# A Mamba mixer inside a MetaFormer kernel: items ahead of the scan, taps by fewer transfers

## The reference

```python
xz = in_proj(normed)                       # x and gate, 1x1
x  = silu(depthwise_conv3x3(x)); g = silu(gate)
xm, z = split(m_in_proj(x))
xm = silu(causal_conv1d(xm, 3 taps) + b)
dt = softplus(xm @ (xp_dt @ dt_w) + dt_b)  # B, C = xm @ xp
h[t] = exp(dt * A) * h[t-1] + dt * x * B   # over 3136 pixels of an image
y = (C . h + D * xm) * silu(z)
out = out_proj(m_out_proj(y) * g)
```

## Time and profile before

| | us |
|---|---|
| median of three runs (3843.79 to 3852.31) | 3848.09 |
| profiled execution | 3854.38 |
| its span | 3852.5 |
| TensorE, VectorE, ScalarE, GpSimd busy | 3198.3, 2774.0, 2555.0, 1635.8 |
| TensorE's granted clock, mean | 0.948 |

### The profile page before, as it was taken

The page is one execution under the profiler, slowest core; times in us unless marked ns, Lnnn a source line. Parts: engine busy times, 40 slices in busy tenths (PEclk is TensorE's granted clock), DMA queues, the critical chain, the costliest instruction groups (busy, mean ns, idle before and its releaser), DMA issues. The chain is left out here.

```text
span 3852.5 us, 71476 instructions
## 1 busy us (share of the span) xinstructions
PE 3198.3 (83%) x20904; PEld 1809.4 (47%) x20904; DVE 2774.0 (72%) x4460; ACT 2555.0 (66%) x4684; POOL 1635.8 (42%) x1502
## 2 busy tenths in 40 slices
PE   5799999978677898989999765877888858688865
PEld 2688888854233343434444321333433324377722
DVE  2566666657408999989999994666999967544456
ACT  4455555559698988989898642785665629644456
POOL 0233333310047888989898863003766730000000
PEclk9899999989898999999999997998999979899979
DMA  4100000012256657574766522220000002410022
GB/s 96 28 14 14 14 14 14 14 27 59 75 140 186 160 165 197 145 200 134 208 160 188 149 64 73 49 51 22 22 21 20 18 22 58 94 39 17 17 54 53
DMA packets 210810, 298.02 MB, mean 77 GB/s; under 512 B 75034, under 2 KB 195150, under 8 KB 210258
## 3 DMA queue, kind: packets, MB, share of 16 engines
q1 hardware_dynamic: 201066, 286.08, 28.7%
q10 hardware_dynamic: 9576, 10.08, 1.1%
HBM read 193.93 MB, written 102.03 MB: 77 GB/s over the span
## 5 line engine op out<-in xcount | busy, mean ns | idle before, releaser
L1586 POOL TENSOR_TENSOR mam_hc<-mam_h,mam_cs 128x896 f32<-128x896 f32 x336 | 703.1, 2093 | 188.0 <-DVE mam_h L1551 87.0
L1551 DVE TENSOR_TENSOR_SCAN mam_h<-mam_a,mam_kept,mam_dbx 128x448 f32<-128x448 f32 x672 | 738.4, 1129 | 24.4 <-ACT mam_a L1437 23.3
L1318 PE MATMUL mam_ps_y<-mam_hc,mam_ident 128*128 128x448 f32 x1344 | 570.3, 558 | 133.1 <-POOL mam_hc L1586 132.9
L1987 POOL TENSOR_TENSOR scan_ch<-scan_h,scan_cs 128x392 f32<-128x392 f32 x256 | 339.8, 1346 | 399.6 <-DVE scan_h L1931 320.6
L1437 ACT ACTIVATE mam_a<-mam_ft,mam_a_neg 128x448 f32<-128x448 f32 x672 | 410.6, 660 | 81.0 <-DVE mam_h L1551 80.3
L1318 PEld LDWEIGHTS mam_ps_y<-mam_hc,mam_ident 128*128 128x128 f32 x1344 | 249.0, 193 | 433.4 <-POOL mam_hc L1586 224.0
L1538 DVE TENSOR_TENSOR mam_dbx<-mam_ps_u,mam_bs 128x448 f32<-128x448 f32 x672 | 381.7, 613 | 35.6 <-DMA mam_bs<-dram_bc 35.6
L766 POOL TENSOR_TENSOR att_prob<-att_prob,att_share 128x588 f32<-128x588 f32 x128 | 151.7, 1185 | 452.0 <-DVE att_share L951 452.0
L418 PE MATMUL f_xc_ff<-all_x,f_centre 128*128 (+1 forms) x256 | 125.9, 575 | 133.1 <-DVE all_x L308 133.1
L886 ACT ACTIVATE att_pt<-att_ps_t 128x512 f32<-128x512 f32 x128 | 76.5, 598 | 209.9 <-PE att_ps_t L827 209.9
L379 ACT ACTIVATE f_h<-f_hid 96x784 f16<-96x784 f32 x256 | 207.1, 811 | 0.0
(11 more groups left out here) (216 smaller groups left out, 7361.8 us busy)
## 6 DMA issues: line engine op xcount, KB each, us to landing
mam_taps<-normed SPq DMA_DIRECT2D x1008, 43.5 KB
mam_bs<-dram_bc SPq DMA_DIRECT2D x28, 896.0 KB, 14.7
mam_cs<-dram_bc SPq DMA_DIRECT2D x28, 896.0 KB, 16.6
mam_ft<-dram_steps SPq DMA_DIRECT2D x42, 448.0 KB, 4.8
normed<-f_staged SPq DMA_DIRECT2D x384, 38.1 KB
f_mixed<-mixed SPq DMA_DIRECT2D x384, 36.8 KB
dram_gs<-mam_gs SPq DMA_DIRECT2D x56, 224.0 KB, 2.1
mam_gt<-dram_gs SPq DMA_DIRECT2D x56, 224.0 KB, 2.7
```

Source lines behind the costliest of these rows:

```text
L1318: mm = pe.matmul(ps_y[p % 2][:, 0:MT], ident[:], hc[t % 2][:, i, :], start=False, stop=(t % 8 == 7 and i == 1))
L1551: dve.tensor_tensor_scan(h[:, n % 8, :], a[t % 3][:, i, :], dbx[:, i, 0:MT], kept[:, at:at + 1], ALU.mult, ALU.add).then_inc(scanned, 1)
L1586: pool.tensor_tensor(hc[t % 2][:], h[:, row:row + 2, :], cs[:, 2 * pair:2 * pair + 2, :], ALU.mult).then_inc(weighed, 1)
L1987: pool.tensor_tensor(out, hd, in_order(cs, 1 - half, d, k), ALU.mult).then_inc(weighed, 1)
```

## The change

`ALONE = 9`. For items 0 to 8, six operations per item go from ScalarE to VectorE, ahead of VectorE's scan: relu of the step (`positive`), the excess over SMALL (`exceed`), the copy of the B/C rows (`copy_rows`), the polynomial (`polynomial`, three operations for ScalarE's two) and the shift of the logarithm (`shift`). Taps come by 8 transfers an item for 18. Taps 0 are issued by ScalarE. win_5 and win_4 have a semaphore of their own and are prepared first; the fold of the step weights, the other weights and ScalarE's first constants are worked after item 0's front. SyncE no longer waits for `prepared` until j = -9. Stage 0's B loads are issued together at j = -2, k = 2, its C loads at j = -1, k = 0.

```diff
+ALONE = 9
+        def tap_rows(first, count, s, image):
+            at = (8 * s + first // 3) * PAD + first % 3
+            return bass.AP(normed.tensor, normed.offset + image * C * PADDED + at,
+                           [[1, count], [PADDED, C], [1, TAP_N]])
+        def bring_taps(eng, m):
+            s, q = divmod(m, DUOS)
+            for i in range(2):
+                for tile, row, first, count in ((taps_5, 0, 0, 3), (taps_5, 3, 3, 2),
+                                                (taps_4, 0, 5, 1), (taps_4, 1, 6, 3)):
+                    eng.dma_start(tile[m % 2][i][C * row:C * (row + count), :],
+                                  tap_rows(first, count, s, 2 * q + i)
+                                  ).then_inc(taps_in[m % 2], 16)
...
                 def load_taps(m):
                     reached(sp, front_b, m - 1)
-                    for i in range(2):
-                        for tap in range(TAPS_5 + TAPS_4):
...
-                            sp.dma_start(tile[m % 2][i][C * row:C * row + C, :],
-                                         normed[2 * q + i, :, at:at + TAP_N]
-                                         ).then_inc(taps_in[m % 2], 16)
+                    bring_taps(sp, m)
...
-                load_taps(0)
-                sp.wait_ge(prepared, n_prep)
...
+                    if j == FIRST + 2:
+                        sp.wait_ge(prepared, n_prep)
...
+                        if j == -2 and k == 2:
+                            for g in range(4):
+                                load_b(0, g)
+                        if j == -1 and k == 0:
+                            for g in range(4):
+                                load_c(0, g)
-                        if (t + 6) % 48 in (0, 2, 4, 6) and 0 <= (t + 6) // 48 < STAGES:
+                        if (t + 6) % 48 in (0, 2, 4, 6) and 0 < (t + 6) // 48 < STAGES:
...
             def _(pe):
-                pe.wait_ge(weights_in, (n_loads + 2) * 16)
...
-                pe.wait_ge(prepared, n_prep)
+                pe.wait_ge(prepared, n_win)
+                def fold():
+                    pe.wait_ge(weights_in, (n_loads + 2) * 16)
+                    pe.matmul(ps_u[0:D, 0:D], wx_dt[:], wdt[:], start=True, stop=True)
...
+                    pe.wait_ge(prepared, n_prep)
...
+                        if k == 2 and front == 0:
+                            fold()
...
             def _(act):
+                bring_taps(act, 0)
+                load_silu(nc)
+                def prepare():
+                    load_exp_and_ln(nc)
+                    act.wait_ge(weights_in, (n_loads + 2) * 16)
...
+                    act.wait_ge(prepared, n_prep)
...
-                    act.wait_ge(exped, m + 1)
-                    act.activation(mag[:], ex[:], ACT.Relu, bias=below).then_inc(excess, 1)
+                    if m >= ALONE:
+                        act.wait_ge(exped, m + 1)
+                        act.activation(mag[:], ex[:], ACT.Relu, bias=below).then_inc(excess, 1)
...
+                def positive(m):
+                    dve.wait_ge(absed, m + 1)
+                    reached(dve, summed, m)
+                    dve.tensor_scalar(rv[:], ps_b[:, 0:MT], dt_b[:, 0:1], 0.0, ALU.add, ALU.max
+                                      ).then_inc(relued, 1)
+                def exceed(m):
+                    dve.wait_ge(exped, m + 1)
+                    dve.tensor_scalar(mag[:], ex[:], -SMALL, 0.0, ALU.add, ALU.max
+                                      ).then_inc(excess, 1)
+                def copy_rows(m):
...
+                    dve.tensor_copy(bcs[:], ps_c[0:HALF, 0:MT]).then_inc(bc_copied, 1)
+                def polynomial(m):
...
+                    dve.tensor_scalar(quad[:], es[:], 1.0 / 3, -0.5, ALU.mult, ALU.add
+                                      ).then_inc(squared, 1)
...
+                    dve.tensor_tensor(quad[:], quad[:], es[:], ALU.mult).then_inc(quads, 1)
...
+                    dve.tensor_scalar(quad[:], quad[:], 1.0, None, ALU.add).then_inc(added_one, 1)
+                def shift(m):
...
+                    dve.tensor_scalar(ln1[:], ln1[:], log_b, None, ALU.add).then_inc(shifted, 1)
+                for m in range(ALONE):
+                    positive(m)
+                    exceed(m)
+                    copy_rows(m)
+                    polynomial(m)
+                    shift(m)
                 make_u(0)
```

More of the change, by code:

```diff
@@ L1063, in mamba_phase @@
         dbx = buf.psum("dbx", [P, 2, BANK])
-        (weights_in, folded, logged0, exp_a, prep, prepared) = (buf.sem(n) for n in (
-            "weights_in", "folded", "logged0", "exp_a", "prep", "prepared"))
+        (win_in, weights_in, folded, logged0, exp_a, prep, prepared) = (buf.sem(n) for n in (
+            "win_in", "weights_in", "folded", "logged0", "exp_a", "prep", "prepared"))
         taps_in = [buf.sem(f"taps_in{p}") for p in range(2)]
@@ L1104, in _ @@
             def _(sp):
-                for tile, name in ((win_5, "mb_win_5"), (bs[0:TAPS_5 * C, 0:1, 0:2 * P], "mb_tap_5"),
-                                   (win_4, "mb_win_4"), (bs[0:TAPS_4 * C, 1:2, 0:2 * P], "mb_tap_4"),
-                                   (win2, "mb_win2"), (cs[:, 0:1, 0:384], "mb_tap1"),
+                for tile, name in ((win_5[:], "mb_win_5"),
+                                   (bs[0:TAPS_5 * C, 0:1, 0:2 * P], "mb_tap_5"),
+                                   (win_4[:], "mb_win_4"),
+                                   (bs[0:TAPS_4 * C, 1:2, 0:2 * P], "mb_tap_4")):
+                    sp.dma_start(tile, w[name]).then_inc(win_in, 16)
+                for tile, name in ((win2, "mb_win2"), (cs[:, 0:1, 0:384], "mb_tap1"),
                                    (win_z, "mb_win_z"), (w_bc, "mb_w_bc"), (wx_dt, "mb_wx_dt"),
@@ L1457, in _ @@
                             save(t - 3)
-                        if k == 1 and previous is not None:
+                        if k == 1 and previous is not None and previous >= ALONE:
                             quadratic(previous)
@@ L1471, in _ @@
                                 activate_z(inner)
-                            load_exp_and_ln(nc)
+                            if front == 0:
+                                prepare()
+                            else:
+                                load_exp_and_ln(nc)
                         elif k == 3 and 0 <= t - 2 < STEPS:
@@ L1476, in _ @@
                             step_logs(inner)
-                        if k == 5 and inner is not None:
+                        if k == 5 and inner is not None and inner >= ALONE:
                             copy_bc(inner)
@@ L1492, in made @@
                     return n_made[0]
+                dve.wait_ge(win_in, 4 * 16)
+                for weights, tap in ((win_5, bs[0:TAPS_5 * C, 0, 0:2 * P]),
+                                     (win_4, bs[0:TAPS_4 * C, 1, 0:2 * P])):
+                    flat = weights[:].rearrange("c i m -> c (i m)")
+                    made(dve.tensor_tensor(flat, flat, tap, ALU.mult))
                 dve.memset(below, -SMALL)
@@ L1498, in _ @@
                 dve.memset(zero, 0.0).then_inc(prep, 1)
+                made(dve.memset(tails[:], 0.0))
                 made(dve.memset(w_dt[:], 0.0))
-                for tile in (tails, kept, yt[0], yt[1]):
+                for tile in (kept, yt[0], yt[1]):
                     made(dve.memset(tile[:], 0.0))
                 dve.wait_ge(weights_in, (n_loads + 2) * 16)
-                for weights, tap in ((win_5, bs[0:TAPS_5 * C, 0, 0:2 * P]),
-                                     (win_4, bs[0:TAPS_4 * C, 1, 0:2 * P])):
-                    flat = weights[:].rearrange("c i m -> c (i m)")
-                    made(dve.tensor_tensor(flat, flat, tap, ALU.mult))
                 made(dve.tensor_tensor(win2[:].rearrange("c t m -> c (t m)"),
@@ L1517, in _ @@
                 dve.wait_ge(folded, 1)
[L1518 removed]
+                dve.wait_ge(prepared, n_win + 2)
                 made(dve.tensor_copy(w_dt[0:D, 0:D], ps_u[0:D, 0:D]))
@@ L1576, in _ @@
             def _(pool):
-                pool.wait_ge(prepared, n_prep)
+                pool.wait_ge(prepared, n_win + 1)
                 def weigh(t):
@@ L1603, in series @@
                 def series(m):
-                    pool.wait_ge(quads, m + 1)
+                    if m < ALONE:
+                        pool.wait_ge(added_one, m + 1)
+                    else:
+                        pool.wait_ge(quads, m + 1)
                     pool.tensor_tensor(es[:], quad[:], es[:], ALU.mult).then_inc(sers, 1)
```

47 lines of the change are left out of this document (24 added, 23 removed).

## The result

The changed kernel takes 3989.53 us, median of four runs (3986.59 to 3996.39), beside 3848.39 for the kernel before (four runs): +141 us, a ratio of 1.0365 with a 95% interval of [1.0345, 1.0385]. Its profiled span is 3989.9 us.

A forecast was written before the change was run, and what follows sets the result against it. Head bound by item preparation, VectorE pacing afterwards; merged taps would confine rows to the first DMA engine. Head 42, start 9, transition 14 and scan 135 sum to +200: 4054 profiled, 4048 us forecast, range 3860 to 4340.

The forecast's parts named there:

- How many engines share a load: Tap loads: the outer count's largest divisor up to 16, from the first engine on; 3 and 2 engines for merged loads.
- The first engine's time for 148 rows: Tap loads of one item: 148 rows of 1856 B at 20.7 GB/s take the first DMA engine 13.3 us.
- The lower bound, 11.2 us: Low end for the first engine's rows of an item, from the densest slice of the weight loads, 24.5 GB/s an engine.
- confined, but mostly hidden: Rival, chance 0.04: the first engine does a row in 60 to 75 ns once its queue is never empty; about 3880 us.
- Head, +42: Before the first scan: an item takes 16.2 us on the first engine against 11.55, over nine items; +23 to +90.
- Start, +9: Phase start: taps 0 ready at 1042.5, taps 1 behind them at 1055.8 against 1046.44; +4 to +14 us.
- Transition, +14: Store of item 7's rows to end of pass 0's steps: 72 us against 57.9; +10 to +27.
- Scan, ordinary items, +35: Items 11 to 55: taps come 3 us late, mostly given back by the h buffers' slack; 1 x 35, 0 to 120.
- Stage changes, +100: Scan: two items at a change need 70.6 us against 43; +20 at each of five changes.
- VectorE's part: Head: six operations moved from ScalarE make its item 8.0 us, with 0.7 us waiting for VectorE's excess.
- The first rival: Rival, chance 0.15: the destination's count decides, 12 or 16 engines a load; -38 us, 3810 us.
- Confined, and the waits add up: Rival, chance 0.04: SyncE stalls on the first engine's full queue; 27 instead of 23.4 us an item over 45 items, 4330 us.

The follow-up runs named there:

- experiment 1: Changed kernel with the tap loads' two outer counts exchanged, 24 channels outermost in the source, weights permuted to match: 3848.20 us, ratio 0.9998 to the kernel before.
- experiment 5: Changed kernel with 24 channels outermost in the tap loads and stage 0's B and C loads back in turn: 3830.69 us, ratio 0.9958 to the kernel before.
- experiment 10: Changed kernel, its narrow tap loads kept, with stage 0's B and C loads back in turn: 3982.97 us, ratio 1.0335 to the kernel before.
- experiment 9: Changed kernel with 24 channels outermost in tap loads, stage 0's B and C in turn, head's zs stored by ScalarE, taps issued earlier: ratio 0.9946 to kernel before.
- experiment 12: Changed kernel, wide taps, B and C in turn, head's zs stored by ScalarE; SyncE stores xm, issues taps, then stores dt: 3823.31 us, 0.9932 of kernel before.
- experiment 6: Changed kernel with 24 channels outermost in the tap loads and ALONE = 0, so VectorE takes nothing: 3843.05 us, ratio 0.9994 to the kernel before.

## Why the prediction was right, and where it was off

The forecast was 4048 us in a range of 3860 to 4340, slower at 0.82; it came to 3989.5. The mechanism was the forecast's, and the size was too large by 59 us: 35 too much for ordinary items of the scan, 21 for the head, 7 for the stage changes, 4 for the start, and 8 too little for the transition. By its own steps:

**How many engines share a load.** Right, and exactly: 3, 2 and 12 (9856 packets). The Trainium skill's rule, in "DMA: Bandwidth & Descriptors", section "Why a DMA increments its semaphore by 16 and not by 1", that the count must divide the slowest dimension of both sides, agrees with this and with experiment 1, where the source's two counts are exchanged and the destination keeps its 72 and 48 partitions: 12 is the largest count up to 16 that divides 24 and 72, or 24 and 48.

**The first engine's time for 148 rows.** This is the term that was mis-sized. I took 20.7 GB/s, 13.3 us; the flat slices show 26 GB/s, so 148 x 71 ns = 10.6 us. The row I took it from, attention's loads, averages unlike packets: in its 4.8 us the rows of 4704 B took 181 ns in the median, which is 26 GB/s as well, and the mean is pulled down by shorter rows and by some packets that took over 300 ns. The 14.7 GB/s of the earlier trace rows came from a stretch in which seven engines were busy in the mean: there a row of 1856 B took 122 ns in the mean, and 149 between 1166 and 1174 us, where all sixteen were busy. The lower bound, 11.2 us, was missed too: it is the mean of sixteen engines in one slice, not the rate of one with rows ready. By the Trainium skill's figure in "DMA: Bandwidth & Descriptors", section "Specifications", about 27 GiB/s an engine, the estimate was 9.5 us; the trace has 1.1 us more. The rival "confined, but mostly hidden" had said 60 to 75 ns a row, which is what was measured; its price was wrong, since at this rate the rows still bind. Its 3880 is also less than its own terms give, 3893 to 3918.

**Head, +42.** Measured 13.9 us an item for 11.6: 9 x 2.3 = +21. With 10.6 in the place of 13.3 the prediction's own sum, 2.9 + 10.6 = 13.5, gives +18.

**Start, +9.** Item 1 came 28.7 us after the phase's start, for 23.9: +4.8. The recorded terms add up to 1042.2 for taps 0, not 1042.5; with 10.6 they put item 1 at 27.5 us after the phase's start.

**Transition, +14.** The rest of the 47.7, some +22 beside a head of nine items. By the step's own ends, from the store of item 7's rows (1159.90) to the end of pass 0's steps (1245.85), it is 86.0 us for 72 forecast and 57.9 before, +28. Up to the first matmul of taps 10 it was right, 34.0 for 31.8, though SyncE stood in their issue for 17.95 us and dt and ft came behind; from there to the first scan too, 10.6 for 10. The steps of pass 0 were not: 41.4 us for 25.5 and 5 of stall. Of VectorE's 21.5 us of waits for decays 18 lie in them, the rest just ahead of the first scan: ScalarE's list stood behind a small store that had been issued behind the C loads, and behind taps 11. The step had 5 for this. Experiments 5 and 10 measure B and C ahead, in single traces: 11.4 us of the stretch with wide loads and 17.2 with narrow ones.

**Scan, ordinary items, +35.** Measured 0: passes of 27.3 us in both. A load issued 14.3 us ahead and taking 10.6 + 2 + 2 is late by 0.3, which the steps' slack may cover. **Stage changes, +100.** Measured +93 in all, for five. With 10.6, 2 x 16.7 + 31.8 = 65.2 against 43 is late by 22, less the 4 of before: +18 each; the mean was 18.6. That the recorded +100 lies so near is in part luck, as its term for the rows was 2.7 us too long.

**VectorE's part.** ScalarE's list of an item as it ran, from the first gate to the end of the table load (only its ends and the wait for VectorE's excess):

```profile
1065.76 0.54 ACT L1395 ACTIVATE mam_xg<-mam_ps_a 64x448 f32<-64x448 f32 x1
...
1071.28 0.58 ACT L1422 ACTIVATE mam_ex<-mam_mag 128x448 f32<-128x448 f32 x1
1072.31 0.67 ACT L1428 ACTIVATE mam_ln<-mam_mag,mam_consts 128x448 f32<-128x448 f32 x1 [0.46 <-DVE mam_mag L1602]
1073.00 1.28 ACT L97 ACT_TABLE_LOAD   x1
```

It is 8.5 us long, 8.0 forecast; the gap is 0.46 us, where 0.7 was taken. The operation itself is right, its worth was not: "the head's item would fall to about 8.7 us" if nothing else changed, a figure for which no working is given. With wide loads it fell to 10.7. Two things had been left out. A load of three shifts costs SyncE 0.8 us to issue and not 0.416, so eight save 1.4 us an item and not 4.2. And SyncE's order makes a loop of its own (experiments 9 and 12). The first rival's 3810 falls with them: had the loads been wide, the answer was 3848, since (10.7 - 8.7) x 9 = 18 us of its gain were missing, and B and C ahead cost 15 where it counted 2 of gain. I had the loss for the right reason and the gain too large.

**Confined, and the waits add up.** Its mechanism was there, 15.7 and 17.95 us for SyncE to issue eight loads behind B and C, at the transition and the stage changes, where the sum had already put its time. In the head it showed too: there the issue took 9.0, 7.2 and 8.0 us at every other item, for 5.4. At ordinary items of the scan, where it was to cost 3.6 us each, it did not, 5.5 us an issue. Its 4330 does not follow from its terms; 45 x 3.6 on top of 4048 is 4210.

## What to carry to other kernels

When DMAs are merged, put a count with a large divisor up to 16 outermost on both sides: here one swap of two counts is worth 141 us at the same bytes and the same number of instructions. Price the merged load by the rows of the busiest engine and by its own issue time, not by the number of loads. And where one engine issues all transfers, ask of each what it keeps waiting behind it: a small store that another engine's next step needs goes ahead of the bulk that nobody wants yet.

## What the runs showed of the hardware

- A DMA engine with rows always ready moved rows of 1856 B at 26 GB/s; two and three of them showed as flat 52 and 78 GB/s. Such a row took 76 ns by its own record while two or three engines worked, and 149 ns in the mean while all sixteen did (kernel before, 1166 to 1174 us, 231 GB/s).
- SyncE's issue time depended on the shape: 0.42 us for 24 rows, 0.8 for three shifts by 24 channels wide, 0.7 for the same narrow. Eight narrow loads took 17.95 us to issue behind 3.7 MB of B and 15.7 at a stage change, although six of the eight use only two or three engines; eight wide ones behind the same 3.7 MB took 6.2. That a queue was full is the likely reason; no trace shows a queue's fill.
- The load that waits for a small store came 13.1 us after it when four loads of 896 KB had been issued ahead of the store, and 2.8 us after it without them.
- TensorE's granted clock between 1041 and 1129 us was 0.92 in the kernel before, 0.83 in the changed one, 0.90 and 0.89 in experiments 1 and 9, and 0.96 in experiment 12. Four matmuls took 3.32 us after a wait for taps and 1.77 without one. Late data are not all of it: experiment 6, which has experiment 1's loads and ScalarE's full list, had 0.97.
